# The last 88 context keys in one transfer, main chunks of 127 or 126 keys, and phase rows padded to 128

## What is computed

```python
def _L0_xattn_ref(query_input, key_input, value_input, Wq, bq, Wk, bk, Wv, bv):
    q = query_input @ Wq + bq
    k = key_input @ Wk + bk
    v = value_input @ Wv + bv
    attn = jnp.einsum('bqd,bkd->bqk', q, k) / scale
    attn = jax.nn.softmax(attn, axis=-1)
    return jnp.einsum('bqk,bkd->bqd', attn, v)

x = x + _L0_xattn_ref(_layernorm(x, axis=-1), ctx_1024, ctx_1024, ...)
x = x + _L0_attn_ref(...)     # a selective scan
x = x + _L0_ffn_ref(...)
x = x + _L1_xattn_ref(...)    # 16 heads, local window
x = x + _L1_attn_ref(...)     # attention with a mask from phases
x = x + _L1_ffn_ref(...)      # 8 experts, the top 2 of them
```

```python
r_embed = qp / jnp.maximum(jnp.linalg.norm(qp, axis=-1, keepdims=True), 1e-12)
quantum_output = _linear(r_embed, Wfq, bfq)
return hidden_states + output + 0.1 * quantum_output
```

## Time and profile before

| | us |
|---|---|
| median of 3 runs | 666.38 |
| lowest, highest | 666.16, 670.92 |
| the profiled execution | 666.37 |
| its span (first to last instruction) | 664.6 |
| what lies around the span | 1.8 |

### The profile page before, as it was taken

The page is one execution under the profiler, slowest core; times in us unless marked ns, Lnnn a source line. Parts: engine busy times, 40 slices in busy tenths (PEclk is TensorE's granted clock), DMA queues, the critical chain, the costliest instruction groups (busy, mean ns, idle before and its releaser), DMA issues. The chain is left out here.

```text
span 664.6 us, 11620 instructions
## 1 busy us (share of the span) xinstructions
PE 603.7 (91%) x4390; PEld 456.9 (69%) x4390; DVE 463.7 (70%) x790; ACT 367.9 (55%) x694; POOL 234.0 (35%) x187
## 2 busy tenths in 40 slices
PE   4999998999998877878788999999999899999997
PEld 4455554454356766767677888887777678889897
DVE  3743333346867999999999517788977868876554
ACT  1311111124988999999999333344656455556343
POOL 2000000000069999999898200025641012231000
PEclk9999999999999999999999999999999989999999
DMA  9999999994912222233320000000100022210000
GB/s 319 399 401 392 392 391 391 394 322 141 268 61 97 95 99 110 99 107 111 113 96 1 1 0 18 1 0 18 36 2 2 2 64 80 64 48 1 33 1 32
DMA packets 31294, 86.47 MB, mean 130 GB/s; under 512 B 8076, under 2 KB 19816, under 8 KB 29064
## 3 DMA queue, kind: packets, MB, share of 16 engines
q1 hardware_dynamic: 31096, 85.67, 36.0%
q10 hardware_dynamic: 144, 0.06, 0.1%
HBM read 83.50 MB, written 1.11 MB: 127 GB/s over the span
## 5 line engine op out<-in xcount | busy, mean ns | idle before, releaser
L761 POOL TENSOR_TENSOR dbu<-du,bs 128x1024 f32<-128x1024 f32 x64 | 149.7, 2368 | 6.7 <-DVE w_in L1009 4.7
L890 ACT ACTIVATE weighed<-T,CT 128x256 f32<-128x256 f32 x222 | 95.0, 593 | 1.3 <-PE T L1088 0.9
L1009 DVE TENSOR_TENSOR_SCAN w_in<-hS,dbu 128x1024 f32<-128x1024 f32 x42 | 94.6, 2271 | 0.4 <-ACT hS L879 0.4
L879 ACT ACTIVATE hS<-delta,negA 128x504 f32<-128x504 f32 x128 | 90.8, 814 | 4.9 <-DVE xn L1009 2.2
L1102 PE MATMUL Y<-ident,weighed 128*128 128x128 f32 x512 | 66.7, 273 | 0.0
L1088 PE MATMUL T<-ident,w_in 128*128 128x128 f32 x336 | 45.9, 279 | 19.8 <-ACT weighed L890 14.3
L1102 PEld LDWEIGHTS Y<-ident,weighed 128*128 128x128 f32 x512 | 57.9, 141 | 0.5
L1088 PEld LDWEIGHTS T<-ident,w_in 128*128 128x128 f32 x336 | 36.0, 140 | 30.7 <-DVE w_in L1009 27.4
L383 POOL COPY w_xp<-w_xp 128x64 f32<-128x64 f32 x3 | 0.6, 234 | 145.6 <-DMA w_out<-in_w_out 145.6
L1009 DVE TENSOR_TENSOR_SCAN xn<-hS,dbu 128x1024 f32<-128x1024 f32 x22 | 50.0, 2274 | 2.3 <-ACT hS L879 2.3
L297 PE MATMUL O<-cN,pT 128*64 128x256 f32 x384 | 46.7, 385 | 5.3 <-DMA cN<-in_ctx 5.3
(11 more groups left out here) (426 smaller groups left out, 1351.3 us busy)
## 6 DMA issues: line engine op xcount, KB each, us to landing
cT<-in_ctxT SPq DMA_DIRECT2D x8, 3202.0 KB, 22.0
cN<-in_ctx SPq DMA_DIRECT2D x8, 3072.0 KB, 24.4
bs<-b_rows SPq DMA_DIRECT2D x32, 512.0 KB, 3.6
raw_w<-in_w SPq DMA_DIRECT2D x16, 256.0 KB, 2.9
w<-in_w SPq DMA_DIRECT2D x7, 256.0 KB, 7.7
vs<-vx SPq DMA_DIRECT2D x8, 136.0 KB, 2.4
x<-in_x SPq DMA_DIRECT2D x2, 512.0 KB, 5.2
cR<-in_ctx SPq DMA_DIRECT2D x8, 128.0 KB
```

What stands on the lines that cost most here:

```text
L761: e.tensor_tensor(dbu[s % NB][:, :, :], half(m.du, s // DS), row, ALU.mult).then_inc(s_bu, 1)
L879: i = e.activation(by_batch(A[s % 2][:, j * HALF:(j + 1) * HALF]), by_batch(m.delta[:, c, h * HALF:(h + 1) * HALF]), ACT.Exp, scale=m.negA ...
L890: i = e.activation(weighed[s % 2][:, q * Q:(q + 1) * Q], T[:, q * Q:(q + 1) * Q], ACT.Copy, scale=c_of(s, q))
L1009: e.tensor_tensor_scan(S[s % NS], A[s % 2][:, :], dbu[s % NB][:, :, :].rearrange("p c n -> p (c n)"), 0.0, ALU.mult, ALU.add).then_inc(s_h, 1)
```

## The change

`load_rest` loads 88 keys, 1513 to 1600, on 88 partitions in one transfer; there is one issue for each tile in place of two. `load_rows` is unchanged and still loads 128 partitions of 12 keys; of these, chunk 0 uses 127 and the chunks 1 to 11 use 126. The transposes make 127 rows for each of these chunks and 88 for the last. `reT` and `wfq` get 128 partitions, of which POOL clears all before the five are filled, so the matmuls of the phases read 128 rows, 123 of them zeros.

```diff
-REST = LK - MAIN
+REST = 88
+CUT = LK - REST
...
-    for rows in (slice(0, 64), slice(64, REST)):
-        e.dma_start(k.cR[r][rows, :, :], k.ctx[2 * i:2 * i + 2, MAIN + rows.start:MAIN + rows.stop, :].rearrange("b p d -> p b d")
-                    ).then_inc(k.s_dR[r], 16)
+    e.dma_start(k.cR[r][:, :, :], k.ctx[2 * i:2 * i + 2, CUT:LK, :].rearrange("b p d -> p b d")).then_inc(k.s_dR[r], 16)
...
         def keys(c):
-            return slice(c, c + (P - 1) * ROWS + 1, ROWS) if c < ROWS else slice(MAIN, LK)
+            return slice(c, c + (P - 2) * ROWS + 1, ROWS) if c < ROWS else slice(CUT, LK)
+
+        def n_turned(c):
+            return P - 1 if c < ROWS else REST
 
         def n_keys(c):
-            return P if c < ROWS else REST
+            return len(range(c, CUT, ROWS)) if c < ROWS else REST
...
-                    j = e.transpose(tps[g % 2][0:n_keys(c), (c % 4) * P:(c % 4 + 1) * P], prob[i % 2][:, keys(c)],
+                    j = e.transpose(tps[g % 2][0:n_turned(c), (c % 4) * P:(c % 4 + 1) * P], prob[i % 2][:, keys(c)],
...
-                    e.wait_ge(k.s_dR[r], 32 * (i // 2 + 1))
+                    e.wait_ge(k.s_dR[r], 16 * (i // 2 + 1))
...
-                        v = cN[r][:, b, c, :] if c < ROWS else cR[r][:, b, :]
+                        v = cN[r][0:n_keys(c), b, c, :] if c < ROWS else cR[r][:, b, :]
...
-                rows = n_keys(c0)
+                rows = n_turned(c0)
...
-            done(e.activation(k.reT[:, 0:HALF], T[0][0:5, :], ACT.Copy), "reT")
+            done(e.activation(k.reT[0:5, 0:HALF], T[0][0:5, :], ACT.Copy), "reT")
...
+            e.memset(k.reT[:, 0:HALF], 0.0)
             e.memset(k.vx[:, :, :, DH:DV], 1.0).then_inc(s_z, 1)
...
-                done(e.activation(reT[:, HALF:TOK], BK[RE][0:5, :], ACT.Copy), "reT")
+                done(e.activation(reT[0:5, HALF:TOK], BK[RE][0:5, :], ACT.Copy), "reT")
...
+            e.memset(reT[:, HALF:TOK], 0.0)
             for h in range(2):
                 e.memset(pb[:, HT * h:HT * (h + 1), :], 0.0).then_inc(s_z, 1)
...
-        k.wfq = sb("wfq", [5, D])
+        k.wfq = sb("wfq", [P, D])
...
-        k.n_w5 = 16 * 8
+        k.n_w5 = 16 * 8 + 1
...
+                e.memset(k.wfq[:, :], 0.0).then_inc(k.s_w5, 1)
...
-        k.reT = k.rows[0:5, 0:4, :].rearrange("p r d -> p (r d)")
+        k.reT = k.rows[:, 0:4, :].rearrange("p r d -> p (r d)")
```

## The result

The changed kernel takes 671.62 us (median of 20 runs, 668.43 to 673.09). The kernel before, run beside it on the same chips, takes 667.38 (20 runs). The ratio is 1.0058, 95% interval 1.0046 to 1.0071: slower by some 4 us, where I had forecast 0.5 us faster, and beyond the 669.5 at which my range ended. The profiled execution of after took 670.37 us against 666.37, so it shows that same difference of 4.0 us and can be read against the one of before row by row.

What follows compares the result with a forecast made beforehand. The prediction took the DMA queue to bound the late cross-attention tiles, with PE's clock halved near 530 us on the chain that ended last. +2.0 for the queue and -2.5 for the clock took 666.37 to 665.9 us, range 663.8 to 669.5.

Steps and rivals of the forecast that it cites:

- Chunks of 127, and 88 in the last: Cross-attention: the new chunk sizes change neither matmul time nor DVE's copy of the last chunk; -0.1 to +0.1 us.
- The columns that stream are the same: Cross-attention chunks: the streamed columns were said not to change, one reason for pricing the new chunk sizes at nothing.
- The bytes of the rest: Cross-attention DMA queue: 46 KB more per tile, six rests ahead of tile 6's `cN`; +2.0 us, 0.7 to 2.7.
- tile 6's values at 138.2 with a wait near 1.9, and a wait in tile 3: Cross-attention: signs that the forecast is right, with PE waiting for `cN`; the kernel before had 136.18 and 1.56 us.
- eleven shares: Cross-attention DMA: 88 rows go as eight on each of eleven engines, 0.33 us a tile, 2.0 us for six.
- The issues, and the clears on POOL: Eight fewer SP issues, -0.1 to 0 us; three POOL clears, covered by other waits, counted 0.
- The padded rows and the clock: Experts' stage start: 128-row phase matmuls keep PE's clock full from 530 to 537 us; -2.5 us, bounds -3.3 and 0.
- by duration the padding is nothing: Phase matmuls: one with 128 rows was said to take as long as one with five.
- idle alone is not it: Clock fall near 530 us: three attention gaps of 1.69, 1.56, 1.56 us kept full clock, so 5-row matmuls were suspected.
- rows don't count: Rival: the clock follows time busy or columns streamed, so it falls again at 530; +2.0 alone, 668.4 us; chance 0.17.
- The sum: Whole kernel: +2.0 for the queue and -2.5 for the clock make -0.5, so 665.9 us.
- Same: Whole kernel: chance 0.92 that the time lies within about 1% (6.7 us) of no change; faster 0.03, slower 0.05.

Runs made afterwards that it cites:

- e10: The changed kernel itself, run once more: 671.81 us, ratio 1.0063 to the kernel before.
- e1: The changed kernel with all transposes of 128 columns again, the surplus column not read: 667.79 us, ratio 1.001 to the kernel before.
- e7: The changed kernel with transposes of 128 columns, the same kernel as e1, run again: 667.33 us, ratio 0.9997 to the kernel before.
- e11: The changed kernel with its padding undone (reT and wfq on five partitions), second run: 673.01 us, ratio 1.0093 to the kernel before.
- e12: The changed kernel without padding and with transposes of 128 columns, leaving the single 88-row transfer and the smaller value chunks: 669.92 us, ratio 1.0045 to the kernel before.
- e2: The kernel before with only the padding (wfq and reT on 128 partitions, three clears): 664.90 us, ratio 0.9963 to the kernel before.
- e8: The kernel before with only the padding, the same kernel as e2, run again: 665.09 us, ratio 0.9977 to the kernel before.
- e6: The changed kernel with transposes of 128 columns and the 88 rows in two transfers, of 64 and 24: 667.02 us, ratio 0.9983 to the kernel before.

## Why the prediction was wrong, step by step

- **"Chunks of 127, and 88 in the last": nothing, -0.1 to +0.1 us.** This is the step that failed. It cost some 13.4 us of PE's time and +4.0 to +4.5 of the kernel's (e10 against e1 and e7; e11 against e12 gives +3.1). I priced the matmul over the values, for which a chunk's keys are rows, and there I was right: 1.95 us for sixteen as before. But the diff also touches the transposes, for which the same keys are the columns of the weight load. "The columns that stream are the same" looked at the 128 columns of `ident` and not at the operand that is loaded. The trace of before had no wide load with an odd number of columns other than the 65 of the last chunk: 133 ns for 65 side by side, where the 128 side by side of L328's transposes take 141 (and 88 take 120 in after). That was the only trace of it, and I had not looked. Since it says nothing of columns 12 apart, the load should have got a bound of its own, as the queue did; none of my rivals had this mechanism.
- **The bytes of the rest: +2.0, 0.7 to 2.7.** The size was about right as a change by itself: +2.2, +2.9 and +3.0 us in three pairs, the last two over my upper end. A part of those two may be clock lost in longer waits: e1's mean granted clock is 0.995 against e2's 0.996, e12's 0.992 against 0.993. In the changed kernel it is hidden: `cN` of tile 6 is there before PE comes for it at 141.44. The forecast "tile 6's values at 138.2 with a wait near 1.9, and a wait in tile 3" looks like what e7 shows (138.39, 1.62 us; 1.80 in tile 3), but it is no proof: e8, with the old rest, has 137.93, 1.83 and 1.82, and the kernel before 136.18. One execution's place cannot carry a term of 2 us. The packet records fit the eleven shares; how much of the cost comes of them is undecided.
- **The issues, and the clears on POOL: 0.** Nothing in the profile of after or in e2 and e8 speaks against it. The clear of the experts' stage takes 0.53 us, and ACT's `pb` waits for DVE, not for it.
- **The padded rows and the clock: -2.5, -3.3 to 0.** Right in direction and in its chain: of the 3.2 us in the profiled pair 2.5 are the clock's, with L2468 4.3 us after the block's start as forecast. The other 0.8 are the matmuls themselves, so "by duration the padding is nothing" was wrong: the two groups of four cost 0.4 us less each with 128 rows. Over many executions the whole is -1.8 and -2.2 on the kernel before, -2.1 to -2.6 on e12 (other chips), and -1.2 on e11. It is less because the fall at that place is not certain in either kernel; that the one profile lost it before and kept it after was luck. My reading of one profile as a rule was too strong, and so was "idle alone is not it" from three gaps that held: e6, e12, e1 and e2 lost the clock behind such gaps. The means of the clock speak against the rival "rows don't count", though e7 did just what it describes.
- **The sum.** The forecast was -0.5, and the kernel is 4.2 us slower. On one chip the steps are +3.0 for the rest (e12), +3.1 for the odd columns (e11) and -1.2 for the padding (e10), together +4.9 there. With the padding first they are -1.8 to -2.2, +2.2 to +2.9 and +4.0 to +4.5. So the odd columns alone cost about the whole loss, 3.1 to 4.5. The price of a part depends on what stands beside it, by 1 us, which is also about what these medians can tell: in the late tiles PE and the queue each hide a part of the other.
- **"Same" at 0.92.** The change, 0.6%, is within the 1% that I called no change, but not for my reasons. The median was outside the range by 2.1 us.

## What to carry to other kernels

When a chunk's size changes, go through every operation that uses it and ask where it is rows and where it is columns: in a transpose the keys are the columns of the weight load. Keep that number even for fp32, above all when the columns are apart as here, if need be by turning a column too many and not reading it (e1: all of the 4 us back for no work). And before pricing an added wait at its full size, ask whether a slower engine elsewhere in the same change will hide it, since then undoing either part alone misleads. A clock that falls in one profiled execution is priced by the mean over executions.

## What the runs showed of the hardware that I had not expected

- An fp32 weight load from columns 12 apart takes 361 ns for 125 columns and 364 for 127, but 217 for 126 and 220 for 128. Side by side it is 152 for 87, 120 for 88.
- The clock's fall changes from one execution to the next of the same code: the same kernel lost it at tile 5 (e1) and at the experts' start (e7), held it behind waits of 2.12 and 2.16 us, and e6 lost it behind one of 1.75. It also fell with PE busy without a gap, inside matmuls of 5 rows (e12, 531.4 us).
- Between other matmuls of 128 rows, four matmuls of 5 rows take 1.06 us until the next one begins, and four of 128 rows 0.68 us.
- A transfer of 96 rows, one of 88, and two of 64 and 24 rows cost the same within 0.4 us in a queue that never rests.
